# A two-layer conditioned linear-attention kernel on one core: h made in front of the keys in every step, first key placings written ahead of query reads, second layer's first two keys in one step, tail with own buffers

## The reference

```python
xn = layernorm(x); q = xn @ Wq + bq; k = xn @ Wk + bk; v = xn @ Wv + bv
# masked tokens: k -> -inf (or -1e6), v -> 0
q = softmax(q, axis=head_dim)
k = softmax(k, axis=tokens)
attn = einsum('bhse,bhsd->bhed', k, v)     # per head a small matrix
y = einsum('bhtd,bhed->bhte', q, attn)
scale, shift = split(silu(emb) @ film_W + film_b, 2)
h = silu(layernorm(y) * (1 + scale) + shift)
x = x + h @ W_out + b_out
```

## Time and profile before

| what | value |
|---|---|
| median of 3 runs | 896.47 us (895.38 to 899.91) |
| profiled execution | 891.59 us, its span 889.8 us |
| busy PE / DVE / ACT / POOL | 846.5 / 680.7 / 608.3 / 553.6 us (95 / 76 / 68 / 62% of the span) |
| DMA | 169.8 MB, 59% of 16 engines' span |

### The profile page before, as it was taken

How to read it: one execution, slowest core, us unless ns; L and a number is a source line. 1 busy time by engine, 2 the same in 40 slices (tenths; PEclk the granted TensorE clock), 3 DMA queues, 4 the chain that set the end, 5 groups by cost and what they waited for, 6 DMA issues and landing times.

```text
span 889.8 us, 19791 instructions
## 1 busy us (share of the span) xinstructions
PE 846.5 (95%) x6581; PEld 715.5 (80%) x6581; DVE 680.7 (76%) x1350; ACT 608.3 (68%) x1445; POOL 553.6 (62%) x743
## 2 busy tenths in 40 slices
PE   4988999999999999999979999999999999999996
PEld 4867788888878788888757888888888888888875
DVE  6977777777777787778768887887788778776754
ACT  6355776776675777777767867776776777767654
POOL 2557667666756557766856776667666766676541
PEclk9989999999999999999989999999999999999999
DMA  8676675766666655555655656556566655665431
GB/s 292 237 257 193 204 237 183 215 206 208 185 208 189 184 204 170 179 171 185 193 170 178 208 173 206 185 174 199 188 193 196 197 190 182 192 197 180 159 119 48
DMA packets 115482, 169.79 MB, mean 191 GB/s; under 512 B 11806, under 2 KB 84630, under 8 KB 115382
## 3 DMA queue, kind: packets, MB, share of 16 engines
...
## 4 chain that ended last, share of the span: by engine, by line
PE 72%; DMA 11%; DVE 5%; ACT 4%; issue 3%; SPq 2%; POOL 2%; ACTq 0%; POOLq 0%; DVEq 0%
PE PS L857 62%; PE PS L946 6%; PE PS L929 3%; DMA qy_turned<-QS 3%; DMA QT<-qy_turned 2%; DMA k_turned<-KT 2%; DMA EK<-k_turned 2%; DMA x_turned<-XS 1%; SPq L392 1%; DMA STAGE<-in_wk 1%; ACT Z L688 1%; ACT XF L740 1%; ACT SK L653 1%; DMA STAGE<-in_wv 1%; SPq L404 1%
## 5 line engine op out<-in xcount | busy, mean ns | idle before, releaser
L565 POOL TENSOR_TENSOR HL<-H,HH 128x512 fp32r<-128x512 f32 x60 | 77.6, 1293 | 206.1 <-ACT HH L721 202.8
L688 ACT ACTIVATE Z<-QT,FC,FA 128x128 f32<-128x128 f32 x240 | 99.1, 484 | 100.0 <-DMA QT<-qy_turned 99.9
L857 PE MATMUL PS<-XH,WH_k 128*128 128x256 f32 x512 | 151.6, 296 | 4.2 <-DVE WL_k L309 4.2
L857 PE MATMUL PS<-XH,WL_k 128*128 128x256 f32 x512 | 146.3, 286 | 0.0
L857 PE MATMUL PS<-XL,WH_k 128*128 128x256 f32 x512 | 146.2, 286 | 0.0
L857 PE MATMUL PS<-WH_o,HH 128*128 128x512 f32 x248 | 105.7, 426 | 14.2 <-issue 11.6
L758 ACT ACTIVATE XN<-X,NBX,RSX 128x512 f32<-128x512 f32 x60 | 48.8, 815 | 91.8 <-POOL NBX L514 91.8
L857 PEld LDWEIGHTS PS<-XH,WH_k 128*128 128x128 f32 x512 | 99.6, 195 | 4.9 <-issue 4.5
L857 PE MATMUL PS<-WH_v,XH 128*128 128x512 f32 x256 | 100.9, 394 | 2.8 <-DVE WL_v L309 2.7
L857 PE MATMUL PS<-WH_q,XH 128*128 128x512 f32 x256 | 100.7, 394 | 0.0
L653 ACT ACTIVATE SK<-SK,KN 128x128 f32<-128x128 f32 x256 | 98.9, 388 | 2.6 <-DVE KN L1149 2.6
...
## 6 DMA issues: line engine op xcount, KB each, us to landing
...
EK<-k_turned SPq DMA_DIRECT2D x128, 128.0 KB, 2.8
...
```

The source lines that it names most:

```text
L565: eng.tensor_tensor(hl_of(o), h_of(o), hh_of(o).bitcast(F32), ALU.subtract).then_inc(pool_hl, 1)
L688: z = eng.activation(Z[:, c * P:c * P + P].rearrange("p (q n) -> p q n", q=Q), src, ACT.Identity, bias=FC[l][:, c, b:b + 1], scale=FA[l][: ...
L857: mm = eng.matmul(dst, left[a](c), right[b](c), start=(c == 0 and a + b == 0), stop=(c == C - 1 and a == 1))
```

## The change

In every step from 4 on, DVE does `h_mul(s-4)` ahead of `keys(s)`, and ACT does `h_high` ahead of `x_turned`. The fold of the conditioning gets the bank `B_TY` in place of a corner of `B_Y`, and its sums stand ahead of `exp_k`. SP's `place_keys` is cut in two, `write_keys` and `place_keys`, and in steps 1 and 3 the write is issued ahead of the read of the queries. At the layer boundary step 32 has the keys of tiles 32 and 33 (the latter in bank `B_TY`), step 33 has none, and the loads and splits of the weights of layer 1 are put elsewhere. In the tail some tiles get buffers and banks of their own (`z_of`, `y_of`, `bank_ty`), the high part of h is made on DVE (`h_parts`) in place of ACT, and the order of all engines is changed.

```diff
--- before.py
+++ after.py
...
@@ -261,11 +260,18 @@
 
         def y_of(o):
 
+            if o == t0 or o == t1:
+                a = 0 if o == t0 else Q // 2
+                return XT[:, a:a + Q // 2, :, :, :].rearrange("p a t c n -> p (a t c n)")
             return XN[:, 1, :] if o == t2 else YN[:, :]
 
+        def z_of(o):
+
+            return BB[:, 2, :] if o in (t0, t2) else Z[:, :]
+
         def bank_ty(o):
 
-            return B_ATT if o == t2 else B_TY
+            return B_ATT if o == t2 else B_K if o == t0 else B_TY
 
         def hl_of(o):
 
@@ -274,6 +280,10 @@
         def hh_of(o):
 
             return XH[0][:, 0:2, :].rearrange("p c n -> p (c n)") if o in (t0, t2) else HH[:, :]
+
+        def bank_k(i):
+
+            return B_TY if i == B + 1 else B_K
 
         def wait_h_free(eng, o):
 
...
@@ -392,10 +402,13 @@
                     eng.dma_start(QT[32 * fq:32 * fq + 32, :, 0:n, :, :].rearrange("p q h c n -> p q (h c n)"), src[fq])\
                        .then_inc(ld_qt[s % 2], 16)
 
-            def place_keys(g):
+            def write_keys(g):
 
                 eng.wait_ge(dve_kt, 2 * g + 2)
                 eng.dma_start(KD[g % 2], KT[:, :, :, :, :].rearrange("p q h a n -> p q (h a n)")).then_inc(st_kd[g % 2], 16)
+
+            def place_keys(g):
+
                 eng.wait_ge(st_kd[g % 2], 16 * (g // 2 + 1))
                 if g > 0:
                     eng.wait_ge(pe_att, 2 * g)
...
@@ -431,18 +442,27 @@
                 write_qy(s)
                 if s == 2:
                     write_x(FIRST)
-                if s > 1:
+                if s <= 3 and s % 2 == 1:
+                    write_keys(s // 2)
+                if s > 3 and s != B - 1:
                     for g in x_pair_at(s):
                         read_x(g)
                 if s == B - 1:
-                    load_second(eng, 5, [0])
+                    load_second(eng, 5, [1, 0, 2, 3])
                 read_qy(s)
                 if s == B - 1:
-                    load_second(eng, 5, [1, 2, 3])
-                    load_second_bias(0, dve_v)
+                    for g in x_pair_at(s):
+                        read_x(g)
                 if s % 2 == 1:
+                    if s > 3:
+                        write_keys(s // 2)
+                    if s == B - 1:
+                        load_second_bias(0, dve_v)
+                        load_second(eng, 6)
+                        load_second_bias(1, dve_q)
                     place_keys(s // 2)
                 if s == NT - 2:
+                    write_keys(NT // 2 - 1)
                     place_keys(NT // 2 - 1)
                 if s == 2:
                     read_x(FIRST)
...
@@ -773,70 +799,73 @@
                     norm_x(7)
                 for n in norm_at(s):
                     norm_x(n)
-                if s == B:
-                    split_high(5)
                 if 0 <= o:
                     film(o)
+                if s in (B, B + 1):
+                    h_high(o)
                 if s >= 3:
                     norm_y(s - 3)
+                if s == B - 1:
+                    split_high(4, [0, 1])
+                if 0 <= o and s not in (B, B + 1):
+                    h_high(o)
+                if s == B - 1:
+                    split_high(4, [2, 3])
+                if s == B:
+                    exp_q(j)
+                    split_high(6)
                 if s == 1:
                     exp_k(1)
                     values(0)
                 if s == 2:
                     norm_x(4)
+                    conditioning_sums(0)
                     exp_k(2)
                     norm_x(5)
                 if s == 3:
                     x_turned(4)
                 if s > 3 and m < NSTEP:
                     x_turned(m)
-                if 0 <= o:
-                    h_high(o)
-                if s == B - 1:
-                    split_high(4)
-                if s == B:
-                    split_high(6)
+                if s >= 3 and s in FILM_SLOTS:
+                    conditioning_sums(FILM_SLOTS.index(s))
                 if s == 0 or s >= 3:
                     exp_k(i)
-                if s in FILM_SLOTS:
-                    conditioning_sums(FILM_SLOTS.index(s))
                 if s == 0:
                     x_turned(2)
                     x_turned(3)
                 if s == 3:
                     x_turned(5)
+                if 0 <= j and s != B:
+                    exp_q(j)
+                for n in keys_at(s):
+                    exp_k(n)
                 if 0 <= j:
-                    exp_q(j)
                     heads(j)
+                if s == B - 1:
+                    split_high(5)
                 if s > 0:
                     values(i)
                 if s == 3:
                     split_high(3)
-                for n in keys_at(s):
-                    exp_k(n)
                 if s == B + 3:
                     split_high(7)
             film(LAST_Y - 1)
+            exp_q(t0)
+            heads(t0)
             h_high(LAST_Y - 1)
             norm_y(t9)
-            exp_q(t0)
...
@@ -865,12 +894,16 @@
                 if i > 0:
                     eng.wait_ge(act_xh, 2 * g + 2)
                     wait_x_low(eng, 2 * g + 2)
-                eng.wait_ge(dve_ka, i)
+                if i == B + 1:
+                    eng.wait_ge(act_cp, len(FILM_SLOTS))
+                    eng.wait_ge(dve_film, len(FILM_SLOTS))
+                else:
+                    eng.wait_ge(dve_ka, i)
                 xs = [lambda c: XH[g % 2][:, c, :], lambda c: XL[g % 2][:, c, :]]
                 for cc in range(2):
                     f = (2 * p + cc) * P
                     ws = [lambda c: WH[0][:, c, f:f + P], lambda c: WL[0][:, c, f:f + P]]
-                    dst = bank(B_K, cc * PAIR, PAIR)
+                    dst = bank(bank_k(i), cc * PAIR, PAIR)
                     mm = split_product(dst, ws, xs, fresh=(4 * l if i % B == 0 and cc == 0 else None))
                 mm.then_inc(pe_k, 1)
 
...
@@ -1008,7 +1042,10 @@
             turn_x(1)
             for s in SLOTS:
                 i, j, o = s, s - 2, s - 4
-                keys(i)
+                if s != B + 1:
+                    keys(i)
+                if s == B:
+                    keys(B + 1)
                 if s == 1:
                     turn_x(2)
                     turn_x(3)
...
@@ -1043,21 +1080,21 @@
                     output(o)
                 if 0 <= j:
                     mix(j)
+            attention(t0)
             values(t2)
-            attention(t0)
+            mix(t0)
+            turn_queries(t1)
             queries(t2)
+            attention(t1)
             turn_y(t9)
-            turn_queries(t1)
-            mix(t0)
-            output(LAST_Y - 1)
-            attention(t1)
-            turn_queries(t2)
             mix(t1)
             turn_y(t0)
+            output(LAST_Y - 1)
+            turn_queries(t2)
             attention(t2)
             mix(t2)
+            turn_y(t1)
             output(t9)
-            turn_y(t1)
             output(t0)
             turn_y(t2)
             output(t1)
...
-            def h_low(o):
-
-                eng.wait_ge(act_hh, o + 1)
+            def h_parts(o):
+
                 eng.wait_ge(dve_h, o + 1)
+                wait_hh_free(eng, o)
+                then(eng.tensor_copy(hh_of(o), h_of(o)))
                 eng.tensor_tensor(hl_of(o), h_of(o), hh_of(o).bitcast(F32), ALU.subtract).then_inc(dve_hl, 1)
 
             def add_x(o):
...
@@ -1336,13 +1374,13 @@
             key_sums(1)
             start_count()
             values(1)
+            turn_keys(1)
             turn_queries(0)
-            turn_keys(1)
             queries(1)
             stat_x(4)
+            keys(2)
             stat_x(5)
             zero_attention()
-            keys(2)
             turn_queries(1)
             values(2)
             turn_x(4)
@@ -1355,72 +1393,72 @@
             turn_keys(2)
             for s in SLOTS[3:]:
                 i, j, o = s, s - 2, s - 4
+                if s == B + 1:
+                    h_mul(o)
                 if s >= 5:
                     add_x(s - 5)
                 if s >= 3:
                     mixed(s - 3)
                 if j == B:
                     second_ones()
-                if s == B:
-                    split_low(eng, 5, LOW_ON_DVE[5])
                 if s == 3:
                     turn_x(6)
                     turn_x(7)
-                if 3 < s < NT - 4:
+                if 3 < s < NT - 4 and s != B:
                     turn_x(s + 4)
                 turn_queries(s - 1)
+                if 0 <= o and s != B + 1:
+                    h_mul(o)
                 keys(i)
-                if 0 <= o:
-                    h_mul(o)
+                if s == B:
+                    turn_x(s + 4)
                 if s >= 3:
                     turn_y(s - 3)
+                if s == B - 1:
+                    split_low(eng, 4, LOW_ON_DVE[4])
```

(38 more changed lines are left out.)

73 lines of the change are left out of this document (36 added, 37 removed).

## The result

The changed kernel takes 938.43 us in the median of 4 runs (934.90 to 946.34), the kernel before 896.21 (895.38 to 899.91); the ratio is 1.0475, with a 95% interval from 1.0402 to 1.0548. It is 4.7% slower, 42 us, and lies outside the range of the prediction (876 to 912).

A forecast was written before the change was run, and what follows sets the result against it. TensorE was taken as the bound, busy 846.5 of 889.8 us. Start -4.7, boundary -5.4, tail -2.5 and steps +12.5 came to no change, 896.5 us against the median 896.5; the range was 876 to 912.

The forecast's parts named there:

- Start: Steps before 5: earlier keys write and placing, and a clock that does not fall, gain 4.7 us.
- Tail: End of the kernel: own buffers and the high part of h on DVE remove waits on ACT, gaining 2.5 us.
- The closed loop: Regular steps: film end, h_mul, keys, turn_y, write, read, film; 12.98 us in layer 1, 13.51 in layer 0, a step's minimum.
- Boundary: Steps 32 and 33: moved keys and earlier weights remove 7.5 us of waits, 2.1 comes back, gaining 5.4 us.
- refill: Step 33, shortened by the moved keys: TensorE waits 2.1 us ahead of mix(31) for heads(31).
- The steps: The 56 steps between: DVE's keys wait for film, closing a loop; 9.7 us lost in layer 0, 2.9 in layer 1, 12.5 taken.
- rival A: Regular steps: legs shorten, layer 0 goes at layer 1's pace, gaining 7.3 us, nothing lost in layer 1; 876.6 us, chance 0.33.
- Rival B: Regular steps: the loop closes at the long pace in both layers, +28.0 us; 911.9 us, chance 0.17.

The follow-up runs named there:

- the first experiment: The changed kernel with h_mul back behind the keys on VectorE in all steps but 33; 881.86 us, ratio 0.9883 to the kernel before.
- high part late: The changed kernel with ScalarE's high part of h behind the pass over turned x again; 913.52 us, ratio 1.0224 to the kernel before.
- the experiment on the start: The kernel before with only the first placing changed: keys turned and written ahead of the queries in step 1; 890.65 us, ratio 0.9981.
- the second experiment: The kernel before with only h_mul moved ahead of the keys on VectorE; 922.8 us, ratio 1.0333.
- KM and KB in PSUM: The changed kernel with the two tiny tiles of the keys' maximum in PSUM in place of SBUF; 914.41 us, ratio 1.0245 to the kernel before.
- turn_y first too: The changed kernel with turn_y, too, ahead of the keys, from step 4 on but 32 and 33; 895.04 us, ratio 1.0028 to the kernel before.

## Why the prediction failed

**Start, right in sum.** The placing was to start at 42.7 and attention(0) at 46.9. After:

```profile
42.64 1.85 SPq L417 DMA_DIRECT2D EK<-k_turned  x4
```

```profile
47.14 0.46 PE L964 MATMUL PS<-EK,VV 128*32 128x32 f32 x32 [1.08 <-DMA EK<-k_turned]
```

The clock did fall, though, for a shorter time. Two windows ahead of and behind that point:

```profile
42.50:48.40 5.90, 4.04 (x53) 3.33 (x51) 5.46 (x13) 4.38 (x14) 3.55 (x7) 1.00 0.80 247
48.40:53.50 5.10, 5.10 (x30) 5.10 (x31) 4.93 (x11) 2.10 (x3) 4.48 (x9) 0.67 0.49 142
```

TensorE had been busy 4.04 of 5.90 us, against 2.63 of 6.00 before. The 0.67 is a mean of the two levels: the granted clock is 0.50 from 48.5 to 51.9 and 1.00 behind that, so it is halved for 3.4 us, where it was for 6.8 before. This and other edits up to step 5 made -4.0 of the predicted -4.7. The placing alone gave 1.8, with the clock halved for 6.8 us as before. What the clock gave is not shown: in the first experiment, whose start is the same, it stays at 1.00 from 42 to 60, but is halved for 6.8 us from 74.0, where the changed kernel has it for 3.4, and step 5 starts at 81.28, no earlier than here. The start is a term with a spread, too: in the other traces with this start step 5 comes between 79.69 and 81.83, and at 83.29 and 84.13 with the high part late.

**Tail, right in sum.** -2.2 against -2.5. The closed loop takes part of it: the stretch from step 62 on is 49.1 us in all seven kernels that have this tail and the keys first, and 50.4 to 50.7 in the four that have h_mul in front.

**Boundary, wrong in size.** "If all goes, it is 2.00+0.7+4.84 = 7.5" and a refill of 2.1. The refill was right in kind, and too small: 3.8 and 3.7 us stand ahead of mix(31) in the changed kernel and in the first experiment, and of the waits in step 32 that I had taken as gone 2.3 and 4.8 us are left. With h_mul behind the keys the pair gained 0.2 us, in the changed kernel 1.9. What the floor of the pair is made of is open. The late landing of step 32's write (6.4 us) is in it, but it was there before (7.0), and the one edit that made it land in 2.9 lengthened the pair. The clock is in it as well, which I had left out of this term: it was halved for 6.8 us in the pair of the kernel before. And the sum hung on one trace, in which the largest of the waits was 4.84; the experiment on the start, with the same code there, has it at 2.69.

**The steps, right in mechanism, wrong in size, and this decided.** The loop was named, and its neighbours too (DVE idle ahead of h_mul in nearly every step: 140.4 us in 55 times in the changed kernel). The term was +12.5; it came out as +51.4, of which 30.5 are h_mul's by the second experiment; the rest, 20.9, is about what the two experiments on the high part of h and on `KB` give back. Two sizes failed.
First, "from the write's issue to the next film 7.94, 8.01 and 6.83, 7.59 in the mean", and 8.12 from two steps in layer 0. Over 24 steps of layer 1 of the kernel before this leg is 7.91 in the mean, and over 25 steps of layer 0 (6 to 30) it is 8.56. With these the sum would have been 3.07+7.91+2.31 = 13.29 and 13.94, which is +12 and +21 and a time near 917. In the changed kernel and the three that come next to it (h_mul alone, high part late, KM and KB in PSUM) the leg is 7.85 to 7.91 in layer 1: it does not shorten there. In layer 0 it does, to 7.82 to 8.25: the slack of rival A was there in layer 0, but only 0.3 to 0.7 us of it, and the loop still stayed above the step. Three rows were too few for a number that is multiplied by 28; a tenth of a us in it is 3 us. The row of 6.83 is the low end of a spread from 6.83 to 8.74, and it comes up again in the changed kernel (6.83 to 8.63).
Second, "from DVE's keys start to the issue of the write 3.07 (h_mul is in it before, and will be)". It was 3.15 where nothing else was changed, and 3.76 in the changed kernel: the high part of h, made earlier on ACT, brought GpSimd's low part onto the keys' small addition. This is the larger of the two: of the 0.96 us by which a step of layer 1 is longer than my 12.98, 0.69 are this leg and 0.27 the one from write to film. I had priced h_high's move at nothing, by the idle time of ACT, and asked nothing about what the engine behind it would then run beside. It lengthened the leg by 0.6 us in each of some 55 steps, and cost 21 to 22 us of the 53 by the two experiments on it; it would be 33 if layer 0 had passed it on in full. That ACT's cover was there I had read from TensorE's waits on ACT, 2.5 us in all, and the loop does not pass through those.

Rival B came nearest (the loop above the step in both layers), with 912 us and a chance of 0.17; its reason, that a later write meets the keys write or the x placings on the queue, is not what the rows show, since the leg from write to film did not grow. Rival A's slack was too small. The Trainium skill's figure in "DMA: Bandwidth & Descriptors", section "Anatomy of one DMA — SWDGE (gpsimd) path", 6.4 us as an estimate for a write and a read, spoke for A. That figure is stated for transfers on the gpsimd path, and these are issued by SyncE. The rows say 7.9 from the issue of the one to the use of the other, and they decide.

**The loop in all kernels.**

| kernel | film end to write | write to film | loop, layer 1 | step, layer 1 | step, layer 0 | ratio |
|---|---|---|---|---|---|---|
| before | 2.59 | 7.91 | open | 12.85 | 13.15 | 1 |
| changed | 3.76 | 7.86 | 13.93 | 13.94 | 13.93 | 1.0475 |
| h_mul alone | 3.15 | 7.85 | 13.32 | 13.32 | 13.80 | 1.0333 |
| KM, KB in PSUM | 3.19 | 7.90 | 13.41 | 13.38 | 13.79 | 1.0245 |
| high part late | 3.17 | 7.91 | 13.39 | 13.42 | 13.62 | 1.0224 |
| turn_y first too | 1.87 | 8.87 | 13.05 | 13.07 | 13.59 | 1.0028 |
| keys first | 2.10 | 8.41 | open | 12.91 | 13.15 | 0.9883 |

The legs are means over 24 steps (36 to 59). In the rows marked open they add up to the step as well, as they must in every row; what tells an open loop is that VectorE starts the keys 3.3 to 3.4 us behind TensorE's start in the mean, and never later than 3.9, where it is 5.7 to 6.7 in the closed ones, anything from 3.9 to 8.6. The steps of the row with turn_y come from an execution 9 us slower than the median of that kernel, so its 13.59 is too long for its ratio.
